# Cross-attention on one core: own engine orders for the first three pairs, and the weights' products moved

## What is computed

```python
mu  = jnp.mean(input, axis=(1, 2), keepdims=True)
var = jnp.var(input, axis=(1, 2), keepdims=True)
xn  = (input - mu) * jax.lax.rsqrt(var + EPS) * gamma[None, :, None] + beta[None, :, None]
q   = jnp.einsum('oc,ncs->nos', Wq, xn) + bq[None, :, None]
kv  = jnp.einsum('od,nds->nos', Wkv, context) + bkv[None, :, None]
att = softmax(einsum('nhqc,nhkc->nhqk', q * scale, k * scale), axis=-1)
y   = jnp.einsum('nhqk,nhkc->nhqc', att, v)
out = jnp.einsum('co,nos->ncs', Wo, y) + bo[None, :, None]
return input + out
```

## Time and profile before

| | us |
|---|---|
| median of 3 runs (lowest, highest) | 728.08 (727.77, 731.11) |
| profiled execution, device time | 729.69 |
| its span | 727.9 |

### The profile page before, as it was taken

How to read it: one execution, slowest core, us unless ns; L and a number is a source line. 1 busy time by engine, 2 the same in 40 slices (tenths; PEclk the granted TensorE clock), 3 DMA queues, 4 the chain that set the end, 5 groups by cost and what they waited for, 6 DMA issues and landing times.

```text
span 727.9 us, 29934 instructions
## 1 busy us (share of the span) xinstructions
PE 670.9 (92%) x11204; PEld 445.4 (61%) x11204; DVE 676.4 (93%) x1124; ACT 620.0 (85%) x2248; POOL 566.5 (78%) x360
## 2 busy tenths in 40 slices
PE   5789999999999999999999999999999999899986
PEld 4556666666666656666665666666566666566564
DVE  1599999999999999999999999999999999999992
ACT  2579888899988889988888998888898888899882
POOL 2478888787888878888887888888788888778872
PEclk9789999999999999999999999999999999999997
DMA  6112222222222222222222222222222222222110
GB/s 123 26 53 74 72 57 65 77 70 70 70 72 62 58 69 70 70 74 60 61 67 70 70 70 70 65 58 69 70 70 72 65 66 56 74 73 60 43 47 23
DMA packets 74814, 47.56 MB, mean 65 GB/s; under 512 B 33748, under 2 KB 74708, under 8 KB 74772
## 3 DMA queue, kind: packets, MB, share of 16 engines
q1 hardware_dynamic: 72848, 46.59, 23.9%
q10 hardware_dynamic: 1924, 0.40, 0.3%
HBM read 25.96 MB, written 4.19 MB: 41 GB/s over the span
## 4 chain that ended last, share of the span: by engine, by line
PE 61%; DVE 16%; SPq 9%; issue 7%; ACT 4%; DMA 2%; DVEq 0%; ACTq 0%
PE z L399 30%; PE fill L365 24%; DVE neg_max L536 7%; SPq L290 6%; DVE probs_t L549 6%; PE z L410 4%; ACT probs L481 4%; PE z L424 1%; DVE y L592 1%; PE z L377 1%; DVE spread L580 1%; SPq L253 1%; SPq L242 1%; DMA x_res<-in_x 1%; DMA wv<-in_L_xattn_Wkv 1%
## 5 line engine op out<-in xcount | busy, mean ns | idle before, releaser
L637 POOL TENSOR_TENSOR probs<-probs,recip 128x1024 f32<-128x1024 f32 x256 | 482.1, 1893 | 127.3 <-DVE recip L542 126.3
L481 ACT ACTIVATE probs<-fill,neg_max 128x256 f32<-128x256 f32 x1024 | 472.7, 487 | 76.5 <-DVE neg_max L536 73.1
L536 DVE TENSOR_REDUCE neg_max<-fill 128x4 f32<-128x1024 f32 x256 | 307.8, 1202 | 15.9 <-PE fill L365 14.6
L365 PE MATMUL fill<-c,t 64*128 64x256 f32 x2048 | 290.1, 404 | 32.5 <-ACT probs L481 27.7
L549 DVE STREAM_TRANSPOSE probs_t<-probs 128x1024 f32<-128x1024 f32 x256 | 310.5, 1222 | 3.0 <-POOL probs L637 0.9
L365 PEld LDWEIGHTS fill<-c,t 64*128 64x128 f32 x2048 | 187.4, 189 | 123.6 <-ACT probs L481 88.7
L399 PE MATMUL z<-probs_t,ctx_keys 32*64 32x256 f32 x8192 | 253.1, 380 | 0.8 <-DVE y L592 0.7
L481 ACT ACTIVATION_READ_ACCUMULATOR probs<-fill,neg_max 128x1 f32 x1024 | 224.5, 219 | 0.0
L399 PEld LDWEIGHTS z<-probs_t,ctx_keys 32*64 32x64 f32 x8192 | 175.1, 131 | 64.9 <-issue 35.0
L490 ACT ACTIVATE t<-z,d_col 128x512 f32<-128x512 f32 x128 | 88.5, 740 | 7.4 <-PE z L377 7.4
L497 ACT COPY z_sb<-z 128x1024 f32<-128x1024 f32 x64 | 61.9, 1032 | 7.8 <-PE z L399 7.8
(11 more groups left out here) (38 smaller groups left out, 108.0 us busy)
## 6 DMA issues: line engine op xcount, KB each, us to landing
ctx_keys<-ctx_turned SPq DMA_DIRECT2D x512, 32.0 KB, 1.8
x<-in_x SPq DMA_DIRECT2D x64, 128.0 KB, 2.8
c<-in_ctx SPq DMA_DIRECT2D x64, 128.0 KB, 2.7
ctx_rows<-in_ctx SPq DMA_DIRECT2D x128, 32.0 KB, 1.8
x_res<-in_x SPq DMA_DIRECT2D x32, 128.0 KB, 2.2
out<-y SPq DMA_DIRECT2D x32, 128.0 KB, 1.8
wq<-in_L_xattn_Wq ACTq DMA_DIRECT2D x2, 128.0 KB
wv<-in_L_xattn_Wkv SPq DMA_DIRECT2D x2, 128.0 KB
```

Of the source, the lines that this page charges most:

```text
L365: mm = pe.matmul(banks[:, o, K * qt:K * qt + K], t[p][r:r + 64, hp, s, 128 * qt:128 * qt + 128], c2[p][r:r + 64, s, :], start=True, stop=True)
L481: ins = act.activation(probs[:, k % SLOTS, g, :], bank[:, K * qt:K * qt + K], ACT.Exp, bias=neg_max[:, k, g:g + 1], accum_out=denom[:, k, ...
L536: dve.tensor_reduce(neg_max[:, k, :], fill[k % PAIRS_OF_BANKS][:, :, :].rearrange("p o (t k) -> p (o t) k", t=QT), AX.X, ALU.max, negate=T ...
L637: pool.tensor_tensor(p, p, recip[:, k, :].unsqueeze(2).broadcast_to([128, 2 * QT, K]), ALU.mult).then_inc(probs_ready, 1)
```

## The change

- Pairs 0, 1 and 2 get lists of their own on PE, ACT, DVE and POOL; all others keep the steady one, and so does SP for all pairs. `work` collects, for each step, the items of every pair that fall into it by that pair's own list.
- Steps up to 4 are unrolled, and the loop begins at step 5, with one turn fewer.
- The key-query products come right behind the first mean's product, their bias products behind the first variance's. The transposes of Wo go behind the first scores, the output-value products behind the second and pair 1's mean, the output biases behind pair 0's eighth scores; all three now write to banks of `z` instead of `fill`.
- Pair 1's second projection stands behind pair 1's first scores instead of ahead of pair 0's eighth.
- Pair 1's context turn (`turn_context`) stands behind its fifth maximum on DVE, not behind its first.
- Wk is loaded first, on ACT's queue; gamma, beta and bq follow the first x on SP's; the value weights go behind the second x and the first context rows.
- PE begins with twelve products of constants into a bank that is overwritten later.
- Smaller moves in pairs 0 to 2 of POOL, ACT and DVE, by the lists.

```diff
+WARM_UP = 12
+
+STEADY = None
...
+PE_ORDERS = {
+    STEADY: (at('scores', 0.00, 1.20, 3.50, 5.03, 7.25, 10.15, 10.92, 13.57)
+             + at('mix', 18.05, 18.82, 20.27, 21.80, 22.56, 24.01, 24.77, 25.46) + at('project_out', 30.26)
+             + at('project_in', -4.39, -3.70) + at('mean', -16.17) + at('var', -14.90)),
+    0: (at('scores', -1.006, -0.588, 2.530, 3.339, 5.430, 9.769, 10.701, 12.533)
+        + at('mix', 17.143, 17.146, 17.554, 17.939, 18.267, 30.587, 31.134, 31.137) + at('project_out', 31.816)
+        + at('project_in', -1.490, -1.293) + at('mean', -16.170) + at('var', -14.900) + at('weights', -0.963, -0.363, 12.972)),
+    1: (at('scores', -2.614, 0.801, 1.351, 1.598, 13.706, 15.162, 15.165, 15.516)
+        + at('mix', 19.513, 19.516, 19.890, 20.014, 21.150, 23.018, 24.093, 24.113) + at('project_out', 29.292)
+        + at('project_in', -3.745, -0.800) + at('mean', -16.460) + at('var', -13.461)),
...
+ACT_ORDERS = {
+    STEADY: (at('exp', 1.93, 3.30, 5.47, 7.40, 9.19, 12.09, 13.89, 15.69) + at('t', -2.54, -0.74, 1.06, 1.48)
+             + at('z', 26.56, 27.29)),
+    0: (at('exp', 11.316, 11.383, 14.877, 14.880, 14.883, 14.917, 14.920, 16.792)
+        + at('t', 10.479, 10.965, 11.097, 11.299) + at('z', 29.679, 29.682) + at('weights', 11.313, 14.861)),
+    1: (at('exp', 1.507, 13.596, 13.665, 13.675, 13.678, 13.695, 13.741, 13.744)
+        + at('t', -1.082, -0.750, 1.442, 1.445) + at('z', 29.070, 29.073)),
+    2: (at('exp', 12.611, 12.796, 12.799, 12.802, 12.880, 13.225, 13.477, 16.214)
+        + at('t', -2.302, -2.269, 9.732, 9.733) + at('z', 27.894, 27.897)),
...
+    STEADY: (at('max', 0.97, 2.25, 4.51, 6.44, 8.23, 11.13, 12.83, 14.59)
...
+             + at('turn_context', 1.89) + at('result', 32.35)),
+    0: (at('max', 1.888, 2.669, 4.858, 7.276, 9.313, 10.167, 10.572, 11.670)
+        + at('recip', 4.708, 5.031, 9.455, 9.814, 10.179, 11.587, 13.102, 19.493)
+        + at('turn', 8.242, 9.679, 10.297, 11.652, 14.483, 18.702, 19.781, 20.338) + at('moments', -28.920)
+        + at('mean_var', -25.790) + at('spread', -15.340) + at('sample_var', -14.190)
+        + at('turn_context', 2.526) + at('result', 31.226) + at('weights', 11.853)),
+    1: (at('max', -1.008, 2.743, 4.034, 6.049, 7.710, 11.782, 11.984, 13.353)
+        + at('recip', 3.530, 4.051, 6.075, 10.094, 11.941, 12.904, 15.055, 17.964)
+        + at('turn', 7.060, 10.754, 10.757, 12.181, 13.239, 14.072, 19.603, 21.755) + at('moments', -25.592)
+        + at('mean_var', -24.385) + at('spread', -12.499) + at('sample_var', -10.944)
+        + at('turn_context', 7.927) + at('result', 32.649)),
...
+POOL_ORDERS = {
+    STEADY: (at('divide', 4.65, 6.75, 8.33, 9.74, 11.15, 13.87, 15.63, 18.38) + at('root', -12.21)
+             + at('norm', -14.90, -9.94)),
+    0: (at('divide', -2.428, 19.520, 19.841, 19.844, 19.847, 19.850, 19.861, 33.070) + at('root', -12.210)
+        + at('norm', -14.900, -9.940)),
+    1: (at('divide', 17.077, 17.080, 17.083, 17.086, 17.089, 17.090, 17.093, 17.568) + at('root', -17.916)
+        + at('norm', -18.337, 3.553)),
...
+def work(pair, orders):
+
+    found = []
+    for n in range(-3, 4):
+        owner = pair.shift(n)
         if owner.exists():
-            yield kind, item, owner
+            found += [(time % UNITS, kind, item, owner) for time, kind, item in orders.get(owner.number(), orders[STEADY])
+                      if time // UNITS == -n]
+    for _, kind, item, owner in sorted(found, key=lambda work: work[0]):
+        yield kind, item, owner
...
-    for c in range(-3, 3):
+    for c in range(-3, 5):
         steps(Pair(0, c))
-    with eng.Fori(0, (NPAIR - 8) // 2) as j:
-        steps(Pair(j, 3))
-        steps(Pair(j, 4))
+    with eng.Fori(0, (NPAIR - 10) // 2) as j:
+        steps(Pair(j, 5))
+        steps(Pair(j, 6))
...
-        qk_weights = [(gamma2[:, :], on_both_halves(gamma))] + [
+        qk_weights = [(wk[:, :, :], Wkv[0:H * C, :].rearrange("(p r) c -> r p c", r=128))] + [
             (wq2[:, :, i, :], Wq.rearrange("(p r) c -> r p c", r=128)) for i in range(2)]
+        qk_vectors = [(gamma2[:, :], on_both_halves(gamma)), (beta_col[:, :], beta.unsqueeze(1)),
+                      (bq_col[:, :], bq.rearrange("(p r) -> r p", r=128))]
         out_weights = [(wo[:, :], Wo), (bv_col[:, :], bkv[H * C:2 * H * C].rearrange("(p r) -> r p", r=128)),
...
-        k_weights = [(wk[:, :, :], Wkv[0:H * C, :].rearrange("(p r) c -> r p c", r=128))]
-        v_weights = [(beta_col[:, :], beta.unsqueeze(1)), (bq_col[:, :], bq.rearrange("(p r) -> r p", r=128))] + [
-            (wv2[:, :, i, :], Wkv[H * C:2 * H * C, :].rearrange("(p r) c -> r p c", r=128)) for i in range(2)]
-        QK_DMAS = len(qk_weights) + len(k_weights)
+        v_weights = [(wv2[:, :, i, :], Wkv[H * C:2 * H * C, :].rearrange("(p r) c -> r p c", r=128)) for i in range(2)]
+        QK_DMAS = len(qk_weights) + len(qk_vectors)
...
-            load_weights(sync, k_weights, qk_loaded)
+            load_weights(sync, qk_vectors, qk_loaded)
             load_c(Pair(0, 0), 0)
-            load_weights(sync, v_weights, weights_loaded)
             load_x(Pair(0, 1), 2)
             load_ct(0)
+            load_weights(sync, v_weights, weights_loaded)
             load_c(Pair(0, 1), 2)
...
+            def warm_up():
+
+                for _ in range(WARM_UP):
+                    pe.matmul(fill[1][:, 1, 0:128], ones[:, :], ones[:, :], start=True, stop=True)
...
-                pe.wait_ge(weights_loaded, 16 * OTHER_DMAS)
-                for p in range(HP):
-                    mm = pe.transpose(fill[1][:, 1, C * p:C * p + C], wo[:, 128 * p:128 * p + 128], ident[0:64, 0:64])
-                mm.then_inc(w_mm, 1)
-
+            def query_key_biases():
                 pe.wait_ge(w_act, 3)
...
-                pe.wait_ge(w_dve, 1)
+            def turn_output_weights():
+
+                pe.wait_ge(weights_loaded, 16 * OTHER_DMAS)
+                pe.wait_ge(consts_ready, 4)
+                pe.wait_ge(t_ready, HP)
+                for p in range(HP):
+                    mm = pe.transpose(z[:, 3, C * p:C * p + C], wo[:, 128 * p:128 * p + 128], ident[0:64, 0:64])
...
             def output_value_products():
                 pe.wait_ge(w_act, 5)
...
+            def output_biases():
+                pe.wait_ge(w_act, 7)
...
-                if pair.first() and k == 0:
-                    pe.wait_ge(w_act, 7)
                 if pair.first() and k == 1:
-                    pe.wait_ge(w_dve, 4)
+                    pe.wait_ge(w_dve, 3)
...
+                for kind, item, owner in work(pair, PE_ORDERS):
                     if kind == "scores":
                         scores(owner, item)
+                    elif kind == "weights":
+                        if item == 0:
+                            turn_output_weights()
+                        elif item == 1:
+                            output_value_products()
+                        else:
+                            output_biases()
                     elif kind == "mix":
...
-                        if owner.first():
-                            if item == 0:
-                                query_key_products()
-                            else:
-                                output_value_products()
+                        if owner.first() and item == 0:
+                            pe.wait_ge(w_dve, 1)
+                        elif owner.shift(-1).first() and item == 1:
+                            pe.wait_ge(w_dve, 4)
                         project_in(owner, item)
                     elif kind == "mean":
                         sum_means(owner)
+                        if owner.first():
+                            query_key_products()
                     else:
                         sum_spreads(owner)
-
-            pe.wait_ge(consts_ready, 4)
+                        if owner.first():
+                            query_key_biases()
+
+            pe.wait_ge(consts_ready, 2)
+            warm_up()
             walk(pe, steps)
...
-                for kind, item, owner in work(pair, ACT_ORDER):
+                for kind, item, owner in work(pair, ACT_ORDERS):
                     if kind == "t":
-                        if owner.first():
-                            if item == 0:
-                                query_key_steps()
-                            elif item == 2:
-                                output_value_steps()
+                        if owner.first() and item == 0:
+                            act.wait_ge(w_dve, 3)
                         query_rows(owner, item)
                     elif kind == "exp":
                         exponentials(owner, item)
+                    elif kind == "weights":
+                        if item == 0:
+                            output_weight_steps()
+                        else:
+                            output_value_steps()
                     else:
                         copy_z(owner, item)
 
```

(74 more changed lines are left out.)

30 lines of the change are left out of this document (14 added, 16 removed).

## The result

| kernel | median us | lowest to highest | ratio to before, 95% interval |
|---|---|---|---|
| before | 728.46 | 727.31 to 732.55 (17) | 1 |
| changed | 731.61 | 729.70 to 735.05 (17) | 1.0035, 1.0020 to 1.0049 |

The change makes the kernel 3.1 us slower by the medians (0.43%), 0.35% by the ratio; 733.5 was forecast, within 728.0 to 737.0. The profiled execution of the changed kernel has a span of 729.8 us against 727.9. In all tables medians are of all executions, while ratios and intervals leave out the four that took 934 to 2212 us.

What follows compares the result with a forecast made beforehand. DVE was taken to bound the steady state, with idle time to win only in the head. First result +3.4 us and PE's restart 2.0 made +5.4 on the median 728.08: 733.5 us, range 728.0 to 737.0.

Steps and rivals of the forecast that it cites:

- (f): Pair 1's context turn on DVE: ends at 53.8 us, residual lands at 71.5, DVE waits 8 us, first result +3.4 us.
- (a) to (e): DVE's lead in the head by pair 1's fifth maximum: 4.7 us won, bounds 2.5 and 7.5.
- (d): Output-weight transposes and value products behind first and second scores: hidden in the exponential's wait, up to 1.5 us, 0.3 taken.
- (e): Pair 1's second projection behind its first scores: DVE idle 5.7 us from the first maximum on, against 5.2.
- The wait swallows every lead: At the first result: DVE's wait for the residual leaves nothing of the 4.7 us won in the head.
- the case of 0.02: Rival at SP's queue: lead of more than 8.1 us, so SP is early enough again; 725 us, chance 0.02.
- The case on record as a larger lead (+3.1): Rival at the first result: wait comes, but PE's restart is covered or lead is 6.5 or more; 731.3 us, chance 0.2.
- the turn before 50: Sign of being wrong: pair 1's context turn on DVE before 50 us, where near 54 was forecast.
- (g): PE stands 8 us before pair 3's spread and restarts at 1.2 GHz; DVE loses about 2.0 us (0 to 3).
- (b): Twelve warm-up matmuls at PE's start, some 5.6 us: fast level for key-query products, worth 1.1 us, 6 in 10.
- (a): Early loads, Wk first on ACT's queue: the wait for them ends at 7.2 us, between 6.5 and 8.
- Unrolling costs nothing to within 0.3: Loop entry: two more pairs unrolled and one turn less change nothing to within 0.3 us either way.

Runs made afterwards that it cites:

- both directions of the experiment: Changed kernel with pair 1's context turn back at 1.89: 722.94 us; kernel before with only that turn moved behind its fifth maximum: 739.64 us.
- the short-unroll kernel: Changed kernel with the loop begun at step 3 as in before: 730.17 us, ratio 1.0014; run again, 730.24 us, ratio 1.0023.

## Why the prediction came out as it did

- **(f) The turn and SP's queue: right.** DVE waits 7.5 us (8 forecast) for the residual behind the sixteen copies; both directions of the experiment agree. The lag from turn to result was 17.7 in the sum and measured 16.8, a little under its lower bound of 16.9: SP took 10.62 for the copies instead of 11.22, and the two x loads were shorter (1.35 instead of 2.13).
- **The lead, (a) to (e): mis-sized, and the term that failed.** 4.7 forecast, 9.0 measured (58.45 less 49.48). Of it, 6.0 us of idle time went before the first maximum (5.2 forecast; it starts at 17.12, forecast 18.1). The rest is (d) and (e), where I had 0.5 us lost and 2.8 were won (DVE idles 2.3 us from its first maximum to the turn, where it idled 5.1): I held that nothing in the chain from the third scores to the seventh changes. In before its scores take 2.08 us. Here PE had the fast level just then (20.45 and 24.86, 1.13 and 1.14 us), and the chain takes 8.8 us (20.45 to 29.29) instead of 10.7. That isn't chance: it takes 8.8 us in eight of the nine traces with the changed head and 9.8 in the ninth, against 10.6 to 10.7 in before and the other kernels with its lists. So the slow stretch of before doesn't belong to the chain as such, as I had read it. What sets the level there, and how the lead divides among the moves of the change, no run shows. In the changed kernel and the variants of it with the turn late, the turn ended at 49.5, 49.7, 50.3, 50.9 and 51.8, so against this trace of before no lead was under 6.7: my upper bound of 7.5 was close to the low end.
- **"The wait swallows every lead" contradicts my own sum.** The turn comes earlier by the lead and takes the residual with it: the first result is at 58.45 less the lead plus the lag, and DVE waits 8 us whatever the lead is. So a lead of 8 doesn't close the wait, as the lower end of the range and the case of 0.02 have it; it only puts the result back where it was in before. The lead measured 9.0, and the wait was 7.5.
- **So the first result came 1.8 us earlier, not 3.4 later,** in the profiled executions. The case on record as a larger lead (+3.1) gives the measured difference, but by luck: the lead was larger still, and the unrolling, put at nothing, made up for it. One of the signs that I had named for being wrong, the turn before 50, came true (it ended at 49.48), and x_res, which I had landing near 71, let the result start at 66.25. The first maximum near 18 (17.12), the idle time of 6 to 9 us and the slow stretch behind it came as forecast.
- **(g) PE's restart: right in size.** 2.0 forecast, 1.9 measured (23.33 less 21.42), 1.8 to 3.2 in the other traces with the wait (23.21, 24.63 and 23.18 at their second result). The granted clock was 0.50 from about 61.4 to 71.6. That the clock alone costs it isn't shown: the scores and mixes above take 1.7 us more at the slow level, but an engine that starts from nothing after 8 us has also lost its lead, and no run keeps one and drops the other.
- **(b) The warm-up: right.** The twenty-four records took 5.49 us (5.6 forecast). The key-query products were at the fast level (16 records in 1.11 us), as in four or five of the eight traces, where I gave 6 in 10. The level fell while the bias products ran (granted clock 0.59 in the stage 10 to 11 us), as I had it. The "some 5 us more" for a level that lasts was too much: about 1 us of it is the key-query products, counted already.
- **(a) The loads** were there at 7.6 instead of 7.2, and the wait for them was ended by the bias vector (0.57 us), which now belongs to them. In six of the nine traces with the changed head the key-query products start only at 8.33 to 8.81, beyond the bound of 8 that I gave; in the two shown above that is after 1.58 and 1.51 us of waiting for the same small load.
- **Unrolling costs nothing to within 0.3: wrong in this kernel.** 3.9 us in the first trace, about 1.4 in the medians, with intervals that overlap. The proof offered, that pairs follow at 21.4 us across the loop's entry, looked at DVE, which had a margin; what grew was SP's time for the copies (to 12.5 at pair 4 in before, already there to be read in SP's rows, against 10.1 later).
- **The tail,** which I held to be untouched, is 2.1 us shorter in the profiled execution. It isn't by the change: the second trace of the same changed kernel has 22.18 and 13.93 for the last two distances, where the first has 21.32 and 12.14 and before 22.11 and 12.92, and from pair 6 to the last result it takes 529.0 us, where the first takes 526.4 and before 528.5. One profile of each kernel can't settle 2 us; the medians do.
- **Chances.** Slower by over 0.5% had 0.74, within 0.5% had 0.18, and 0.35% by the ratio it is. The sign was right, and the size 3.1 instead of 5.4.

## What to carry to other kernels

When an order is changed on one engine, follow every item in it that another in-order queue waits for, here one 0.4 us instruction with twenty-two transfers between it and the residual: put behind four more maxima it took back more than all that the other moves had won (with the turn early the kernel is 6.7 us faster than before, with it late 3.1 us slower). Count the issue time of a transfer queue as that of an engine (SP is issuing for some 16 of each 21.4 us), and keep the head item of such a queue as early as its inputs allow. A head that is to be shortened should not pay with a second one: here a wait of 7.5 us on the vector engine let the matmul engine stand until its clock fell, and the pair behind it took 1.9 us more.

## What the hardware showed that I had not expected

- The queue of SyncE isn't independent of the other engines' code: sixteen copies take 10.09 to 10.14 us to issue in the steady turns of every trace, and up to 13.5 us while the compute engines run code for the first time, at the head and again at the tail. The two kernels that unroll one side alone (one trace each) tell SyncE's own new code from that of the others.
- PE's level in the head differs from execution to execution of one and the same kernel: in the two traces of the short-unroll kernel the fast level returned at 16.6 and at 18.9 us, the key-query products took 1.11 and 1.97 us, and the context turn ended 2.1 us apart. I take this for part of the 5.4 us between the fastest and the slowest execution of the changed kernel; that isn't shown.
- The granted clock reads 1.00 at the start of every trace, also where the durations are those of the slow level (in before until 23 us, with a projection of 2.08 us at 20.01). It should be checked against a repeated instruction: scores take 1.13 or 2.08 us.
